# Rotary attention rows in two fp32r parts on half the array each, and a score tile of 640 keys cut as 384 + 256

## The chip, the core and the metric

The kernel runs on one core of a Trainium2 chip. The metric is the device time of one execution in microseconds (us). TensorE (PE in the rows, its weight loads PEld) multiplies, VectorE (DVE), ScalarE (ACT) and GpSimd (POOL) do the rest, and SyncE (SP) issues nearly all DMAs. The on-chip memory is SBUF, and TensorE writes to PSUM, which has 8 banks of 512 fp32 columns on 128 partitions.

## What is computed

A layer on x of 1024 tokens by 512 channels: a rotary attention of 32 heads of 16 channels, a feed-forward with experts, an attention with linear position biases (32 heads of 128, 8 key heads), and the feed-forward again, each with a residual. The change touches the first and, in one detail, the third.

```
def attention_fwd(x, wq, wk, wv, wo, n_heads=32):
    xq = rotary_pos_emb((x @ wq.T).reshape(B, T, n_heads, hd))
    xk = rotary_pos_emb((x @ wk.T).reshape(B, T, n_heads, hd))
    scores = jnp.einsum('bqhd,bkhd->bhqk', xq, xk) * scale
    scores = jnp.where(causal[None, None], scores, NEG_INF)
    probs = jax.nn.softmax(scores.astype(jnp.float32), axis=-1)
    out = jnp.einsum('bhqk,bkhd->bqhd', probs, xv).reshape(B, T, C)
    return out @ wo.T
```

## The kernel before

Products need nearly fp32 accuracy. [...] The kernel has these stages, one after the other:

**Rotary projection** (`rotary_projection_block`, L538, to about 131 us). For each of 8 token tiles TensorE makes q, k and v in 36 matmuls of 512 columns. ScalarE and VectorE apply the rotation into `rot`. The rotated rows are cut in three bf16 parts by casts and subtractions on ScalarE and VectorE (L671, L705, L675, L708), each part is transposed (L634, 24 transposes a tile), copied to `stage`, and stored to DRAM (`parts`) for two tiles at a time by SP (L581). From there SP loads them back into rows for scoring (L462): the rows of one head stand on 96 partitions, which hold the six products of parts in `A_TERMS`. Ones in three more partitions of `k_st` are made by GpSimd (L474), and the negated row maxima go into the same partitions of `q_st`, so a score matmul of 99 rows gives the score less its maximum.

**First maxima** (`FirstMaxima`). Heads go in 8 groups of 4. Row maxima of a group come from score pieces of up to 512 keys, 48 in a group: one matmul of 96 rows (L486, in the next stage L886), a matmul that adds the causal mask where the piece has the diagonal (L489, L889), and a VectorE reduction (L509, L989). Group 0 is done here.

**Rotary attention** (`rotary_attention_block`, L728, about 164 to 434 us). For each group 20 steps (`A_STEPS`). In a step TensorE scores one head's key blocks in a pair of banks (L914, and L918 for masks), ScalarE takes the exponent (L978), then come the products with v (`mix`, L932, four heads at once, each on 32 of the array's columns), and then the pieces for the maxima of the next group, on three banks (4, 5, 7). VectorE reduces the pieces. The order on TensorE is written out by hand; a piece waits until the reduction of the third piece before it has freed its bank, a score until the exponent two steps back is done:

```
for tau in range(NGA * S + 3):
    score(tau)
    ... mix(gg, k, n)
    ... piece(g + 1, n)
```

**Stream** (`stream_block`, about 434 to 1650 us): 64 steps of a token tile and a key head with 4 heads each. The keys of a tile are cut in spans of up to 512 by `key_spans`; a span of 128 is computed as 256 columns, since `score` takes `k0 = min(k0, k1 - 2 * P)`. VectorE adds the bias and takes the maximum of each span (L1754) in two banks. A feed-forward closes the kernel.

Of the kernel before, what the change touches and what calls it, by code (L numbers as in the profile page):

```python
# [411 lines left out]
A_PARTS = 3  # L412
A_ROWS = 6 * DA
A_UNITS = GA * NT
A_LINKS = 5
A_TERMS = ((0, 0), (0, 1), (0, 2), (1, 0), (1, 1), (2, 0))
A_PIECES = [(hh, i, c, span) for hh in range(GA) for i in range(NT) for c, span in enumerate(key_spans(i))]
A_FIRST = sorted(A_PIECES, key=lambda piece: piece[1])


class FirstMaxima:
# [5 lines left out]
    def __init__(self, nc, ctx, own, credited, const, ps, parts_dram):  # L427
# [7 lines left out]
        rows = sb("first_rows", [P, 4, GA * T], BF16)  # L435
        self.rows = rows
        self.q_st = [rows[:, 2 * b, :].rearrange("p (h t) -> p h t", h=GA) for b in range(2)]
        self.k_st = [rows[:, 2 * b + 1, :].rearrange("p (h t) -> p h t", h=GA) for b in range(2)]
# [3 lines left out]
        self.max_rest = sb("max_rest", [P, A_UNITS])  # L442
        self.max_part = sb("max_part", [P, A_PARTS, A_UNITS], BF16)
        self.max_rows = sb("max_rows", [P, P], BF16)
# [6 lines left out]
    def raw_weights(self):  # L451
        flat = self.rows[:, :, :].rearrange("p b n -> p (b n)").bitcast(F32)
        return [flat[:, k * 3 * C:(k + 1) * 3 * C] for k in range(KC)]

    def load_rows(self, queue, b, h, sides=(0, 1)):
        cols = slice(2 * h * P, 2 * (h + 1) * P)
        rows = [self.parts_dram[a].rearrange("(n g h d) t -> n g d h t", n=2, g=NGA, h=GA) for a in range(A_PARTS)]
        for s, (qa, ka) in enumerate(A_TERMS):
            at = slice(s * DA, (s + 1) * DA)
            for dst, n, a in ((self.q_st[b], 0, qa), (self.k_st[b], 1, ka)):  # L460
                if n in sides:
                    queue.dma_start(dst[at, :, cols], rows[a][n, b][:, :, cols]  # L462
                                    ).then_inc(self.loaded[1] if b else self.rows_in[h], 16)

    def store_max(self, sp):
        sp.wait_ge(self.credited["max_out"], 1 + 1)
        for a in range(A_PARTS):
            sp.dma_start(self.q_st[0][A_ROWS + a:A_ROWS + a + 1, :, :],
                         self.max_rows[a * A_UNITS:(a + 1) * A_UNITS, :]).then_inc(self.max_in[0], 16)

    def make_ones(self, pool):

        for b in range(2):
            pool.memset(self.k_st[b][A_ROWS:A_ROWS + A_PARTS, :, :], 1.0).then_inc(self.ones_made, 1)  # L474
            pool.wait_ge(self.ones_made, b + 1)

    def score_pieces(self, pe):
        pe.wait_ge(self.made, 2)
        for n, (hh, i, c, (k0, k1)) in enumerate(A_FIRST):
            if hh == 0 and c == 0 and i % 2 == 0:  # L480
                pe.wait_ge(self.rows_in[i // 2], 16 * 2 * len(A_TERMS))
# [4 lines left out]
            last = pe.matmul(out, self.q_st[0][0:A_ROWS, hh, i * P:(i + 1) * P], self.k_st[0][0:A_ROWS, hh, k0:k1],  # L486
# [6 lines left out]
    def turn_max(self, pe):  # L493
        pe.wait_ge(self.credited["link"], 1 + A_LINKS)
        pe.transpose(self.ps[0:A_PARTS * A_UNITS, 4, 0:P // 2].bitcast(BF16),
                     self.max_part[:, :, :].rearrange("p a u -> p (a u)"),
                     self.const["ident_bf"][:, :]).then_inc(self.credited["max_turned"], 1)
# [7 lines left out]
    def max_of_pieces(self, dve):  # L505
        for n, (hh, i, c, (k0, k1)) in enumerate(A_FIRST):
            u = hh * NT + i
# [4 lines left out]
    def split_max(self, dve, start=1, pieces_done=None):  # L512
# [6 lines left out]
        dve.scalar_tensor_tensor(self.max_rest[:, :], self.row_max[:, :], -1.0, self.max_part[:, 0, :],  # L519
                                 ALU.mult, ALU.subtract).then_inc(link, 1)  # L520
        dve.wait_ge(link, start + 3)
        dve.tensor_copy(self.max_part[:, 1, :], self.max_rest[:, :]).then_inc(link, 1)
        dve.wait_ge(link, start + 4)
        dve.tensor_tensor(self.max_part[:, 2, :], self.max_rest[:, :], self.max_part[:, 1, :],
                          ALU.subtract).then_inc(link, 1)

    def take_max(self, dve):
        dve.wait_ge(self.credited["max_turned"], 1 + 1)
        dve.tensor_copy(self.max_rows[0:A_PARTS * A_UNITS, :],
                        self.ps[0:A_PARTS * A_UNITS, 4, 0:P // 2].bitcast(BF16)).then_inc(self.credited["max_out"], 1)  # L530


def rotary_projection_block(nc, ctx, norm, weights, xt_h, xt_l, w_h, w_l, v_all, o_all, spare, stage_room, first, const, ps, parts_dram, x_in):
# [4 lines left out]
    with ExitStack() as own:  # L538
        def sb(name, shape, dt=F32):
# [5 lines left out]
        part = spare[:, 0:3 * 2 * C].bitcast(BF16).rearrange("p (b a n) -> p b a n", b=2, a=3)  # L545
        stage = [half.rearrange("p (a m t) -> p a m t", a=3, t=2 * P)
                 for half in (sb("stage", [P, 3 * 2 * KC * 2 * P], BF16)[:, :], stage_room.bitcast(BF16))]
# [4 lines left out]
        high_done = sem("high_done")  # L552
        rest1_done = sem("rest1_done")
        mid_done = sem("mid_done")
        low_done = sem("low_done")
        transposed = sem("transposed")
        staged_dve = sem("staged_dve")
        staged_act = sem("staged_act")
# [3 lines left out]
        def take_part(eng, copy, done, i, a):  # L562

            n = 3 * i + a
            eng.wait_ge(transposed, n + 1)
            if i % 2 == 0 and i >= 4:
                eng.wait_ge(stored[i // 2 % 2], 16 * 6 * (i // 4))
            copy(stage[i // 2 % 2][:, a, :, (i % 2) * P:(i % 2 + 1) * P],
                 ps[:, 6 + n % 2, :].bitcast(BF16).rearrange("p (m t) -> p m t", t=P)).then_inc(done, 1)
# [5 lines left out]

# [1452 lines left out]
```

## Time and profile before

| | us |
|---|---|
| median of 3 runs (1671.64 to 1673.54) | 1672.65 |
| the profiled execution | 1671.7 |
| its span | 1669.6 |
| TensorE busy | 1534.6 |
| VectorE busy | 1132.8 |
| ScalarE busy | 828.7 |
| GpSimd busy | 393.5 |

The profile is that of one execution. In its rows, a matmul's duration is modelled up to its last result, so matmuls overlap in time: the time that one takes from the engine is read from start to start.

### The profile page before, as it was taken

The numbers are of one execution on the slowest core, as the hardware profiler recorded it, in microseconds if no ns is written. First come the engines' busy times: TensorE is split into PE (matmuls) and PEld (weight loads), VectorE is DVE, ScalarE is ACT, GpSimd is POOL, SyncE is SP. The second block draws the span as 40 slices with busy tenths as digits, with TensorE's granted clock in tenths as the row PEclk, the third lists the DMA queues.
The fourth block names the chain that finished last, engine by engine and source line by source line (L and its number), as shares of the span: only waits on it lengthen the run. The fifth ranks groups of instructions, "written<-read, shape, count | busy, mean of one in ns | idle before, by whom it ended". The sixth has DMA issues, their size and how long they took to land. (4 is left out here: it accounts for less than half of the span.)

```text
span 1669.6 us, 25633 instructions
## 1 busy us (share of the span) xinstructions
PE 1534.6 (92%) x9096; PEld 1187.5 (71%) x9096; DVE 1132.8 (68%) x2845; ACT 828.7 (50%) x2104; POOL 393.5 (24%) x356
## 2 busy tenths in 40 slices
PE   3885999999898799999999999999999999999969
PEld 2772444443587688888888888888888888888757
DVE  5547777774375478677677677667767767867855
ACT  2451555556432455555555555556555555555521
POOL 4100100001253231322223133133133133131130
PEclk9996999999998899999999999999999999999979
DMA  3143533321100100100000010010010010000011
GB/s 144 38 115 93 73 40 39 43 36 53 44 27 1 38 14 14 39 7 20 14 26 26 1 38 26 1 39 26 1 38 26 1 39 14 13 1 1 1 45 51
DMA packets 42656, 54.56 MB, mean 33 GB/s; under 512 B 6304, under 2 KB 24992, under 8 KB 42528
## 3 DMA queue, kind: packets, MB, share of 16 engines
q1 hardware_dynamic: 41568, 52.52, 12.7%
q8 instruction: 73, 1.20, 0.3%
q10 hardware_dynamic: 960, 0.39, 0.1%
q14 instruction: 55, 0.45, 0.1%
HBM read 44.31 MB, written 8.39 MB: 32 GB/s over the span
## 5 line engine op out<-in xcount | busy, mean ns | idle before, releaser
L1649 ACT ACTIVATE prob<-prob,ab_neg_max 128x128 f32<-128x128 f32 (+7 forms) x256 | 201.5, 787 | 250.5 <-DVE ab_neg_max L1754 249.4
L1771 DVE TENSOR_TENSOR ab_pt_l<-ps,ab_pt_h 128x512 fp32r<-128x512 f32 x288 | 197.8, 687 | 74.0 <-ACT ab_pt_h L1677 73.1
L1677 ACT CAST ab_pt_h<-ps 128x512 fp32r<-128x512 f32 x288 | 171.6, 598 | 111.7 <-PE ps L1562 111.1
L1754 DVE CUSTOM_DVE_ANT_0 prob<-ps,rel 128x512 f32<-128x512 f32 (+3 forms) x256 | 150.3, 587 | 109.2 <-PE ps L52 108.5
L989 DVE TENSOR_REDUCE ra_part_max<-ps 128x1 f32<-128x128 f32 (+1 forms) x336 | 164.8, 550 | 49.7 <-PE ps L889 31.9
L50 PE MATMUL ps<-ab_w_h,ab_xt_h 128*128 128x512 f32 (+1 forms) x512 | 186.2, 364 | 4.3 <-DVE ab_v_l L1791 3.5
L1562 PE MATMUL ps<-ident,prob 128*128 128x128 f32 x1152 | 173.5, 273 | 5.8 <-DVE ab_qt_l L1763 4.5
L52 PE MATMUL ps<-ab_w_h,ab_xt_l 128*128 128x512 f32 (+1 forms) x512 | 173.9, 340 | 0.0
L51 PE MATMUL ps<-ab_w_l,ab_xt_h 128*128 128x512 f32 (+1 forms) x512 | 173.3, 338 | 0.0
L1779 DVE TENSOR_SCALAR prob<-prob,ab_recip 128x128 f32<-128x128 f32 (+7 forms) x256 | 165.8, 648 | 9.1
L1459 POOL TENSOR_TENSOR ab_rms<-ab_ms_eps,neg_half 128x5 f32<-128x5 f32 x64 | 77.7, 1214 | 341.1 <-DVE ab_ms_eps L1796 340.4
L1562 PEld LDWEIGHTS ps<-ident,prob 128*128 128x128 f32 x1152 | 138.1, 140 | 27.5 <-DVE ab_qt_l L1763 5.8
L978 ACT ACTIVATE ra_pt<-ps 128x1024 f32<-128x1024 f32 x96 | 97.3, 1024 | 103.6 <-PE ps L918 91.4
L50 PE MATMUL ps<-ab_kt_h,ab_qt_h 128*128 128x512 f32 (+2 forms) x384 | 135.5, 353 | 5.0 <-DVE ab_neg_max L1754 4.9
L52 PE MATMUL ps<-ab_kt_h,ab_qt_l 128*128 128x512 f32 (+2 forms) x384 | 134.1, 349 | 0.0
L51 PE MATMUL ps<-ab_kt_l,ab_qt_h 128*128 128x512 f32 (+2 forms) x384 | 133.8, 348 | 0.0
L50 PE MATMUL ps<-ab_pt_h,ab_v_h 128*128 128x512 f32 x288 | 128.0, 444 | 6.0 <-DVE ab_pt_l L1771 3.7
L1468 POOL CAST ab_o_h<-ab_o_raw 128x512 fp32r<-128x512 f32 x64 | 41.5, 649 | 348.1 <-ACT ab_o_raw L1691 314.0
L51 PE MATMUL ps<-ab_pt_l,ab_v_h 128*128 128x512 f32 x288 | 113.6, 395 | 0.0
L52 PE MATMUL ps<-ab_pt_h,ab_v_l 128*128 128x512 f32 x288 | 113.6, 394 | 0.0
L50 PEld LDWEIGHTS ps<-ab_w_h,ab_xt_h 128*128 128x128 f32 x512 | 97.4, 190 | 21.9 <-DVE ab_v_l L1791 8.3
L50 PE MATMUL ps<-wo,ab_o_h 128*128 128x512 f32 x256 | 102.6, 401 | 7.6 <-POOL ab_o_l L1470 7.6
(252 smaller groups left out, 3501.9 us busy)
## 6 DMA issues: line engine op xcount, KB each, us to landing
f_raw<-in_wqkv SPq DMA_DIRECT2D x32, 384.0 KB, 3.7
f_raw<-in_wbo SPq DMA_DIRECT2D x32, 256.0 KB, 2.6
ra_first_rows<-in_wa SPq DMA_DIRECT2D x4, 768.0 KB, 10.1
parts<-pa_stage SPq DMA_DIRECT2D x12, 256.0 KB, 3.4
parts<-f_raw SPq DMA_DIRECT2D x12, 256.0 KB, 3.4
ra_q_st<-parts SPq DMA_DIRECT2D x24, 128.0 KB, 6.1
ra_k_st<-parts SPq DMA_DIRECT2D x24, 128.0 KB, 6.7
ra_first_rows<-parts SPq DMA_DIRECT2D x24, 128.0 KB, 6.6
```

The costliest lines, as they stand in the source:

```text
L50: pe.matmul(out, lh, rh, start=start, stop=False)
L51: pe.matmul(out, lh, rl, start=False, stop=False)
L52: return pe.matmul(out, ll, rh, start=False, stop=stop)
L978: act.activation(pt[k % 3][:, h, :], pair.rearrange("p a b -> p (a b)"), ACT.Exp).then_inc(exped, 1)
L989: dve.tensor_reduce(part_max[:, c, u:u + 1], ps[:, PIECE_BANKS[n % len(PIECE_BANKS)], 0:k1 - k0], AX.X, ALU.max).then_inc(piece_max, 1)
L1459: pool.tensor_tensor(rms[:, t % 2, :], ms_eps[:, t % 2, :], const["neg_half"][:, 0:GB + 1], ALU.pow).then_inc(rms_ready, 1)
L1562: last = pe.transpose(ring_bank("p", u, j)[:, h * P:(h + 1) * P], prob[:, u % 2, h, j * P:(j + 1) * P], const["ident"][:, :])
L1649: act.activation(prob[:, t % 2, h, 0:w], prob[:, t % 2, h, 0:w], ACT.Exp, bias=neg_max[:, t % 2, h, pieces_per_head(t % NT) - 1:pieces_per ...
L1677: act.copy(pt_h[:, n % PT, :], ring_bank("p", u, j)).then_inc(pt_high, 1)
L1754: dve.tensor_tensor_reduce(out=prob[:, t % 2, h, k0:k1], in0=ps[:, n % 2, a:b], in1=const["rel"][:, SLIDE - i * P + k0:SLIDE - i * P + k1] ...
L1771: dve.tensor_tensor(pt_l[:, n % PT, :], ring_bank("p", u, j), pt_h[:, n % PT, :].bitcast(F32), ALU.subtract).then_inc(emptied, 1)
L1779: dve.tensor_scalar(prob[:, t % 2, h, 0:w], prob[:, t % 2, h, 0:w], recip[:, t % 2, h:h + 1], None, ALU.mult).then_inc(normed, 1)
```

## The change

The rotated q and k rows are kept in two fp32r parts in place of three bf16 ones, with three products of parts. A head's rows then take 48 partitions, 50 with the maxima, and a group's even heads stand on partitions 0 to 63 and its odd heads on 64 to 127. Scores and pieces become fp32r matmuls on 64 rows of the array. In each step the pieces are no longer given after the mix but in turn with the score blocks, and `piece_slots` chooses them so that they are of the other half; the masks, which use all 128 rows, follow each pair. The projection transposes `rot` itself in fp32 (8 transposes a tile) and makes the parts when it empties PSUM. `make_ones` fills whole `k_st` tiles. In the stream a tile of 640 keys is cut as 384 + 256 in place of 512 + 128.

```diff
-A_PARTS = 3
-A_ROWS = 6 * DA
+A_PARTS = 2
+A_TERMS = ((0, 0), (1, 0), (0, 1))
+A_ROWS = len(A_TERMS) * DA
+A_HALF = P // 2
-A_LINKS = 5
-A_TERMS = ((0, 0), (0, 1), (0, 2), (1, 0), (1, 1), (2, 0))
+A_LINKS = 3
+A_LOADS = 16 * 4 * len(A_TERMS)
+A_STORES = 16 * 2 * A_PARTS
-A_FIRST = sorted(A_PIECES, key=lambda piece: piece[1])
+A_FIRST = sorted(A_PIECES, key=lambda piece: (piece[1], piece[2]))
+def head_rows(st, hh, n):
+
+    at = A_HALF * (hh % 2)
+    return st[at:at + n, hh // 2, :]
+def store_maxima(queue, dst, max_rows, done):
+    for a in range(A_PARTS):
+        for r in range(2):
+            at = A_HALF * r + A_ROWS + a
+            src = a * A_UNITS + r * (A_UNITS // 2)
+            queue.dma_start(dst[at:at + 1, :, :].bitcast(F32), max_rows[src:src + A_UNITS // 2, :].bitcast(F32)).then_inc(done, 16)
...
         for b in range(2):
-            pool.memset(self.k_st[b][A_ROWS:A_ROWS + A_PARTS, :, :], 1.0).then_inc(self.ones_made, 1)
+            pool.memset(self.k_st[b][:, :, :].bitcast(F32), 1.0).then_inc(self.ones_made, 1)
...
             def turn(i):
-                pe.wait_ge(low_done, i + 1)
-                for a in range(3):
-                    n = 3 * i + a
...
-                    for m in range(2 * KC):
-                        last = pe.transpose(ps[:, 6 + n % 2, m * 64:(m + 1) * 64].bitcast(BF16),
-                                            part[:, i % 2, a, m * P:(m + 1) * P], const["ident_bf"][:, :])
+                pe.wait_ge(rot_done, i + 1)
+                for n in range(2):
+                    if i:
+                        pe.wait_ge(staged_low, 2 * (i - 1) + n + 1)
+                    for m in range(KC):
+                        last = pe.transpose(ps[:, 6 + n, m * P:(m + 1) * P],
+                                            rot[:, i % 2, (n * KC + m) * P:(n * KC + m + 1) * P], const["ident"][:, :])
                     last.then_inc(transposed, 1)
...
+            def take_high(i):
+                stage_free(act, i)
+                for n in range(2):
+                    act.wait_ge(transposed, 2 * i + n + 1)
+                    act.copy(staged(i, n, 0).bitcast(F32R),
+                             ps[:, 6 + n, :].rearrange("p (m t) -> p m t", m=KC)).then_inc(staged_high, 1)
...
+def piece_slots(slots):
+
+
+    by_tile = sorted(A_PIECES, key=lambda piece: (piece[1], piece[2]))
+    queues = [[p for p in by_tile if p[0] % 2 == 1], [p for p in by_tile if p[0] % 2 == 0]]
+    order, ends = [], [0]
+    for t in range(slots):
+        queue = queues[t % 2]
+        left = len(range(t, slots, 2))
+        size = sum(k1 - k0 + W // 4 for _, _, _, (k0, k1) in queue)
+        taken = 0
+        while queue and taken * left < size:
+            order.append(queue.pop(0))
+            k0, k1 = order[-1][3]
+            taken += k1 - k0 + W // 4
+        ends.append(len(order))
+    return order, ends
...
+            def mask_piece(n):
+                hh, i, c, (k0, k1) = PIECES[n]
+                if k1 == P * (i + 1):
+                    pe.matmul(ps[:, PIECE_BANKS[n % len(PIECE_BANKS)], k1 - k0 - P:k1 - k0], const["ident_bf"][:, :],
+                              mask[:, :], start=False, stop=True).then_inc(piece_scored, 1)
...
+                for x in range(max(len(blocks), len(pieces))):
+                    if x < len(blocks):
+                        m, j, q0, col = blocks[x]
                         own_keys = kind != "full"
...
+                        last = pe.matmul(out, head_rows(k_st[b], h + m, ROWS)[:, j * P:(j + 1) * P],
+                                         head_rows(q_st[b], h + m, ROWS)[:, half * W + q0:(half + 1) * W],
                                          start=True, stop=not own_keys)
+                    if x < len(pieces):
+                        piece(group, pieces[x])
+                    if x < len(blocks):
                         if own_keys:
                             last = pe.matmul(out[:, 0:P], mask[:, :], const["ident_bf"][:, :], start=False, stop=True)
+                        if x == len(blocks) - 1:
+                            last.then_inc(scored, 1)
+                    if x < len(pieces):
+                        mask_piece(pieces[x])
...
+def score_spans(i):
+
+    w = P * (i + 1)
+    at = min(w, W if w - W != P else W - P)
+    return [(0, at)] + ([(at, w)] if w > at else [])
```

Three places show how instructions move on TensorE. The first is step 1 of a middle group in the rotary attention (half 0, head 1, with the masks of its three key blocks); the column count at a row's end is that of the moving operand. Before, the score blocks with their masks come first, then two mixes, then the pieces:

```order
L914 MATMUL ps<-ra_q_st,ra_k_st 128x512
L918 MATMUL ps<-ident_bf,ra_mask 128x128
L914 MATMUL ps<-ra_q_st,ra_k_st 128x384
L918 MATMUL ps<-ident_bf,ra_mask 128x128
L914 MATMUL ps<-ra_q_st,ra_k_st 128x128
L918 MATMUL ps<-ident_bf,ra_mask 128x128
L932 MATMUL ps<-ra_pt,ra_v 32x128 x4
L932 MATMUL ps<-prob,ra_v 32x256 x4
L886 MATMUL ps<-ra_first_rows 128x384
L889 MATMUL ps<-ra_mask,ident_bf 128x128
L886 MATMUL ps<-ra_first_rows 128x512
```

In the changed kernel the same step (L916 is the score matmul, L881 the piece, L923 and L890 the masks, L940 the mix) reads:

```order
L916 MATMUL ps<-ra_q_st,ra_k_st 128x512
L881 MATMUL ps<-ra_first_rows 128x128
L923 MATMUL ps<-ident_bf,ra_mask 128x128
L890 MATMUL ps<-ra_mask,ident_bf 128x128
L916 MATMUL ps<-ra_q_st,ra_k_st 128x384
L881 MATMUL ps<-ra_first_rows 128x512
L923 MATMUL ps<-ident_bf,ra_mask 128x128
L916 MATMUL ps<-ra_q_st,ra_k_st 128x128
L881 MATMUL ps<-ra_first_rows 128x512
L923 MATMUL ps<-ident_bf,ra_mask 128x128
L940 MATMUL ps<-ra_pt,ra_v 32x128 x4
L940 MATMUL ps<-prob,ra_v 32x256 x4
```

Each score block now has a piece behind it, both on 64 rows of the array, and behind these a mask or two on 128 rows. The masks stand between the pairs.

The second place is the projection between two tiles. Before:

```order
L50 MATMUL ps<-a_w_h,wo 128x512
L51 MATMUL ps<-a_w_l,wo 128x512
L52 MATMUL ps<-a_w_h,a_xt_l 128x512
L634 MATMUL ps<-ident_bf,prob 128x128 x24
L50 MATMUL ps<-a_w_h,wo 128x512
```

In the changed kernel `L631 MATMUL ps<-ident,prob 128x128 x8` stands where the row of 24 stood, and the rows around it are the same.

The third is the score of a tile of 640 keys in the stream. Before, the head's two spans, with a part of the projection between them:

```order
L50 MATMUL ps<-ab_kt_h,ab_qt_h 128x512
L51 MATMUL ps<-ab_kt_l,ab_qt_h 128x512
L52 MATMUL ps<-ab_kt_h,ab_qt_l 128x512
...
L50 MATMUL ps<-ab_kt_h,ab_qt_h 128x256
L51 MATMUL ps<-ab_kt_l,ab_qt_h 128x256
L52 MATMUL ps<-ab_kt_h,ab_qt_l 128x256
```

In the changed kernel the first three rows have 384 columns and the last three stay at 256. That is so for 32 heads, 96 matmuls in all; no row of the stream moves to another place.

## Rows read from the trace of the kernel before

**Rows 1.** The page: the span, and TensorE's busy time, share and instructions.

```profile
span 1669.6 us, 25633 instructions
PE 1534.6 (92%) x9096; PEld 1187.5 (71%) x9096; DVE 1132.8 (68%) x2845; ACT 828.7 (50%) x2104; POOL 393.5 (24%) x356
```

**Rows 2.** Windows: length, busy PE, PEld, DVE, ACT, POOL, PEclk, DMA share, GB/s.

```profile
192.00:226.00 34.00, 32.35 (x267) 14.82 (x265) 25.80 (x59) 19.51 (x22) 0.61 (x1) 1.00 0.38 48
396.00:432.00 36.00, 31.65 (x277) 12.34 (x275) 2.15 (x8) 26.14 (x30) 3.71 (x4) 1.00 0.19 61
```

**Rows 3.** Waits from 200 to 360 us: total us, times, longest.

```profile
PEld ps L886 <- DVE ra_part_max L989: 47.9, 97, 0.8
```

**Rows 4.** Timeline, TensorE: start, us, instruction, count.

```profile
258.13 0.22 PE L889 MATMUL ps<-ra_mask,ident_bf 128*128 128x128 bf16 x1
258.19 0.60 PE L914 MATMUL ps<-ra_q_st,ra_k_st 99*128 99x512 bf16 x2
258.72 1.07 PE L932 MATMUL ps<-prob,ra_v 128*32 128x512 f32 x8
259.71 0.60 PE L914 MATMUL ps<-ra_q_st,ra_k_st 99*128 99x512 bf16 x2
260.25 1.06 PE L932 MATMUL ps<-prob,ra_v 128*32 128x512 f32 x8
```

**Rows 5.** Timeline, TensorE: fp32 transposes, then bf16 scores.

```profile
244.96 0.60 PE L941 MATMUL ps<-ident,ra_o_rows 128*128 128x128 f32 x4
245.41 0.38 PE L914 MATMUL ps<-ra_q_st,ra_k_st 99*128 99x512 bf16 x1
```

**Rows 6.** Timeline, VectorE; then a group of lines (ScalarE): count, busy us, mean ns.

```profile
149.07 9.12 DVE L509 TENSOR_REDUCE ra_part_max<-ps 128x1 f32<-128x512 f32 x16 [4.03 <-PE ps L486]
L978 ACT ACTIVATE ra_pt<-ps 128x1024 f32<-128x1024 f32 x54 | 54.9, 1024 | 41.6 <-PE ps L918 35.1 <-PE ps L914 6.4
```

**Rows 7.** Timeline, TensorE, in the projection between two tiles.

```profile
68.97 0.40 PE L52 MATMUL ps<-a_w_h,a_xt_l 128*128 128x512 f32 x1
69.20 1.07 PE L634 MATMUL ps<-ident_bf,prob 128*128 128x128 bf16 x16
70.61 0.62 PE L634 MATMUL ps<-ident_bf,prob 128*128 128x128 bf16 x8 [0.34 <-DVE pa_stage L568]
71.04 0.48 PE L50 MATMUL ps<-a_w_h,wo 128*128 128x512 f32 x1
71.36 0.40 PE L51 MATMUL ps<-a_w_l,wo 128*128 128x512 f32 x1
```

**Rows 8.** Timeline, GpSimd, VectorE and TensorE, ahead of the second tile.

```profile
35.40 0.54 DVE L158 TENSOR_SCALAR prob<-x,an_mean_var,an_rstd 128x512 f32<-128x512 f32 x1
39.79 7.41 POOL L474 MEMSET ra_first_rows<- 3x4096 bf16 x2
44.27 3.22 DVE L158 TENSOR_SCALAR prob<-x,an_mean_var,an_rstd 128x512 f32<-128x512 f32 x1
50.61 0.50 PE L50 MATMUL ps<-a_w_h,wo 128*128 128x512 f32 x1 [1.40 <-DVE a_xt_l L163]
```

**Rows 9.** Timeline, SP's queue: start, us of issue, DMA, count.

```profile
77.08 4.14 SPq L581 DMA_DIRECT2D parts<-pa_stage  x6
124.81 11.11 SPq L462 DMA_DIRECT2D ra_first_rows<-parts  x24
136.01 4.23 SPq L581 DMA_DIRECT2D parts<-f_raw  x6
142.95 5.48 SPq L462 DMA_DIRECT2D ra_first_rows<-parts  x12
```

**Rows 10.** Timeline, TensorE, in the stream.

```profile
800.18 0.39 PE L52 MATMUL ps<-ab_w_h,ab_xt_l 128*128 128x512 f32 x1
800.41 0.28 PE L50 MATMUL ps<-ab_w_h,ab_xt_h 128*128 128x256 f32 x1
800.53 0.28 PE L51 MATMUL ps<-ab_w_l,ab_xt_h 128*128 128x256 f32 x1
```

More of the change, by code:

```diff
@@ L485, in score_pieces @@
             last_span = k1 == P * (i + 1)
-            last = pe.matmul(out, self.q_st[0][0:A_ROWS, hh, i * P:(i + 1) * P], self.k_st[0][0:A_ROWS, hh, k0:k1],
+            last = pe.matmul(out, head_rows(self.q_st[0], hh, A_ROWS)[:, i * P:(i + 1) * P],
+                             head_rows(self.k_st[0], hh, A_ROWS)[:, k0:k1],
                              start=True, stop=not last_span)
@@ L598, in _ @@
             weights.split_low(pool)
-            pool.wait_ge(weights.w_low, KC)
             first.make_ones(pool)
@@ L795, in pieces_before @@
         def pieces_before(t):
[L797 to L802 removed]
+            return PIECES_TO[min(t, LAST_PIECE)]
         def jobs_at(tau, lag):
@@ L849, in _ @@
         def _(pool):
+            for b in range(2, A_BUFS):
+                pool.memset(k_st[b][:, :, :].bitcast(F32), 1.0).then_inc(ones_made, 1)
+                pool.wait_ge(ones_made, b + 1)
             for b in range(2):
@@ L883, in piece @@
                     pe.wait_ge(max_out, count(1, g, 0))
-                out = ps[:, PIECE_BANKS[n % len(PIECE_BANKS)], 0:k1 - k0]
                 last_span = k1 == P * (i + 1)
-                last = pe.matmul(out, q_st[b][0:A_ROWS, hh, i * P:(i + 1) * P], k_st[b][0:A_ROWS, hh, k0:k1],
-                                 start=True, stop=not last_span)
-                if last_span:
-                    last = pe.matmul(out[:, k1 - k0 - P:k1 - k0], const["ident_bf"][:, :], mask[:, :],
-                                     start=False, stop=True)
@@ L891, in piece @@
-                last.then_inc(piece_scored, 1)
+                last = pe.matmul(ps[:, PIECE_BANKS[n % len(PIECE_BANKS)], 0:k1 - k0],
+                                 head_rows(q_st[b], hh, A_ROWS)[:, i * P:(i + 1) * P],
+                                 head_rows(k_st[b], hh, A_ROWS)[:, k0:k1], start=True, stop=not last_span)
+                if not last_span:
+                    last.then_inc(piece_scored, 1)
+            def mask_piece(n):
[3 more added lines that the diff above has]
+                              mask[:, :], start=False, stop=True).then_inc(piece_scored, 1)
@@ L900, in score, with score_and_pieces @@
+            def score_and_pieces(tau, group, pieces):
                 g, t = tau // S, tau % S
                 b = g % A_BUFS
-                k, h = A_STEPS[t]
-                kind, half, _ = A_SETS[k]
-                if t == 0:
-                    pe.wait_ge(max_in[b], 16 * A_PARTS * (g // A_BUFS + 1))
-                    pe.wait_ge(ones_made, min(g, A_BUFS - 1) + 1)
-                pe.wait_ge(exped, 1 + max(0, tau - 1))
-                for m in range(2 if kind == "rest" else 1):
-                    for j, q0, col in blocks_a(k):
-                        n = W - q0
+                blocks = []
+                if g < NGA:
+                    k, h = A_STEPS[t]
+                    kind, half, _ = A_SETS[k]
+                    if t == 0:
+                        pe.wait_ge(max_in[b], A_STORES * (g // A_BUFS + 1))
+                    pe.wait_ge(exped, 1 + max(0, tau - 1))
+                    blocks = [(m, *block) for m in range(2 if kind == "rest" else 1) for block in blocks_a(k)]
+                for x in range(max(len(blocks), len(pieces))):
+                    if x < len(blocks):
+                        m, j, q0, col = blocks[x]
@@ L946, in _ @@
                 piece(1, n)
+                mask_piece(n)
             for tau in range(NGA * S + 3):
-                g, t = tau // S, tau % S
-                if g < NGA:
-                    score(tau)
+                g, t = (tau + SHIFT) // S, (tau + SHIFT) % S
+                score_and_pieces(tau, g + 1, range(pieces_before(t), pieces_before(t + 1)) if g + 1 < NGA else ())
+                if g + 1 < NGA and t == MAX_AT:
+                    turn_max(g + 1)
                 for gg in range(NGA):
```

219 lines of the change are left out of this document (82 added, 137 removed).

## Prediction

> **What bounds the kernel now.** I read the page first: TensorE is busy 92% of the span, VectorE 68% [rows 1]. Then the windows by stage, since most of the change lies in the rotary attention. In a middle group's 34.0 us (its rows repeat after that time) TensorE is busy 32.35 and VectorE 25.80; in the last group, which has no pieces, 31.65 of 36 us and 2.15 [rows 2]. So TensorE bounds the groups by its work. The view of waits shows the rest: pieces wait 97 times, 47.9 us in all, for a bank that VectorE frees [rows 3], each for at most 0.8 us. A step is bound by TensorE or, where it has many pieces, by VectorE.
>
> TensorE's prices, from start to start. Two score matmuls of 512 columns take 0.53 us in front of a mix and 0.54 behind one; a 128-column mask takes 0.06 (258.13 to 258.19); the mix of a key block, four heads side by side on 32 columns of the array, takes 0.99 (258.72 to 259.71) [rows 4]. I count bf16 at 0.215 for 512 columns. Then two scores should take 0.43; so the change to the mix's shape and back costs the 0.10 behind the scores, and 0.99 less 0.85 (8 records of 512 fp32 columns, two to each quarter, at two cycles a column and 2.4 GHz) is 0.14: 0.24 for a round trip. A change of type alone costs nothing: four fp32 transposes take 0.45, and the bf16 score follows at once [rows 5]. An fp32r matmul takes 0.23 for 512 columns and 0.12 for 256 [rows 10], or 0.32 where its weight load shows (71.04 to 71.36) [rows 7].
>
> Check on before: per group, scores and pieces have 36,864 columns (15.5 us), 64 masks 3.6, mixes 7.7, ten visits to mixes 2.4, transposes 0.9: 30.1, where 32.35 is busy by modelled ends. If each of the 20 steps takes the larger of TensorE's work, VectorE's reductions (16 in 9.12 us, so about 0.57 for the widest, and less for narrower ones) and ScalarE's exponent (1.02) [rows 6], it is 33.1. Measured is 34.0, so 0.9 is waiting between.
>
> **The change in the groups.** *What it removes.* A piece and a score of opposite halves could run at once. Summed over the order, with the longer of each pair, 36,864 columns become 26,496. At fp32r's 0.45 us per 1000 that is 11.9 in place of 15.5: 3.6 us less a group, if the halves overlap. No row shows two row halves at once; the nearest is the mix, where four column quarters take 0.99 for 4096 fp32 columns on all of them, so they do overlap [rows 4].
>
> *What it adds.* The masks use all 128 rows. In a group there are 55 places of a pair (or a single matmul); behind 43 of them stands a mask, so the array goes from halves to full rows and back 43 times. No row shows that change. Bounds: below nothing, as with a change of type [rows 5]; above 0.33, the mix's 0.24 [rows 4] and 0.09 of exposed fp32r weights [rows 7]. The nearest row is the mix's: a change of the array's shape between two plain matmuls. I take 0.24 each, less 0.12 at the ten mixes, whose own change is then partly made already: 43 × 0.24 − 1.2 = +9.1 on TensorE. TensorE's sum becomes 26.5 + 9.1 = 35.6 against 30.1.
>
> The Trainium skill ("TensorEngine Tiling (Array Packing)", Tiling Modes, Key Properties) says that tiles run independently, and that changing the tiling mode, not just the tile, drains TensorE. The trace agrees for the mix's columns (the 0.24 above); no row here shows it for rows.
>
> *What else moves.* VectorE's reductions are as many as before, 24.3 us a group, ScalarE's as well. The pieces now come with the scores, not behind the mix: a piece that waits for VectorE holds the score blocks behind it, then the mix, and by `scored` the exponent, so ScalarE starts later. Step by step with the larger of the three engines, a group gives 32.0 us at a price of 0, 33.3 at 0.10, 35.0 at 0.16, 37.7 at 0.24, 41.3 at 0.33, against 33.1 for before. So the sign turns near 0.09 by steps and near 0.11 by TensorE's sum (3.6 + 1.2 over 43) where VectorE covers nothing; the waits of the 0.9 that may go raise it to about 0.17. The forecast: +2.6 (before's gap of 3.9 between sum and measured vanishes by two thirds as TensorE fills up: 35.6 + 1.0 − 34.0) to +4.6 (37.7 − 33.1), taken +3.6 a group, ×7 = **+25**.
>
> The last group has no pieces to overlap, and its masks still change the mode. By steps: 25.1 before, 25.3 at 0, 29.9 at 0.24, 32.8 at 0.33: **+4.8**.
>
> fp32r of 128 columns: 16 pieces and some scores a group. No row shows one below 256 columns. Below it costs nothing, since most stand beside a wider partner; above, if 128 cost what 256 does (0.12 [rows 10]), 16 × 0.06 on singles, at most +0.4 a group. I take nothing.
>
> **Projection and first maxima.** 24 bf16 transposes start at 69.20 and, with a break, end before 71.04: 1.84 us [rows 7]. Eight fp32 ones take twice the 0.45 of four [rows 5]: 0.9. That is −0.94 a tile, −6.6 for seven tiles on TensorE.
>
> GpSimd's two memsets (3 × 4096 bf16) take 7.41, 0.90 ns a column. Beside them VectorE's `tensor_scalar` takes 3.22 in place of 0.54, and TensorE waits for that chain [rows 8]. After, two of 2048 fp32 columns: I take the price by columns, 3.7, so −3.7. If it goes by bytes, 7.4: nothing gained.
>
> But SP's queue nearly fills the time too: stores to loads 6.94 (136.01 to 142.95), 24 loads 11.11, together 18.05 [rows 9]. The parts grow from 1.5 to 2 MB for two tiles (4 stores of 512 KB), the loads stay 24: about 8.0 + 11.1 = 19.1, more than TensorE's new pair of tiles (its rounds take 58.93/3 = 19.64 now [rows 9], less 1.9). So SP sets the end. First stores: 77.08 − 3.7 − 1.9 − 3.1 (one pass less on each of ScalarE and VectorE before the parts are there, about 1.0 each for 1024 columns [rows 6], and one hand-over of about as much, an estimate) = 68.4; three rounds of 19.1 put the last ones at 125.7 against 136.01. Then one longer store, +1, and in the first maxima mode changes +1 and four stores of maxima for three, less two links, 0: **−8**. Bounds: −2 (memset by bytes and no shorter chain) to −11.
>
> **Stream.** 96 matmuls lose 128 columns of fp32r: 0.23 − 0.12 for 256 [rows 10], so 0.055 to 0.057 each. TensorE bounds there; the later span is unchanged and VectorE's two maxima become more even. **−5.4** (bounds −6 to 0).
>
> **Sum.** 25 + 4.8 − 8 − 5.4 = +16.4 on the profiled execution's own 1671.7: 1688; the median of the runs is 1 us above it, so 1689.
>
> **Rivals.** (a) *The halves' change is free, and pairs overlap.* For it: type changes are free [rows 5], and a half array stays two halves of the same columns, unlike the mix. Against it: rows 4. A group then changes by −1.1 (steps), −3.6 (TensorE's sum) or, with the 0.9 and better spread pieces, −4.7. With −13.4 outside and 0 in the last group: 1651, 1634, 1626; centre 1638. This ends on the other side, and decides below a price of about 0.10.
>
> (b) *About half the price, 0.12:* the modelled 0.10 in front of the mix [rows 4] is all, and the way back hides under the next weights. +0.7 a group by steps, +2.3 last: 4.9 + 2.3 − 13.4, less up to 3 for freed waits: 1665 (1650 to 1675).
>
> (c) *Dearer:* 0.33, with fp32r weights exposed (+7.3 × 7 + 7.7 − 13.4 = +45, 1717), or halves that don't overlap: at 0.24 a group gives 41.2, and about the same time. Against it: in a step of 1.7 us VectorE's and ScalarE's work covers part.
>
> The Trainium skill ("TensorE: Matmul & The Clock Gate", Part 3) gives a measured speedup of 3.07 for four row tiles at 512 columns. By a like share (0.77 of ideal), two halves would save less than the 3.6 above, about 2.3; no row here shows it.
>
> **How the numbers follow.** Forecast (0.24; 1675 to 1708): 0.42. (a) 0.32, (b) 0.16, (c) 0.10. The range leaves out the dearest part of (c) and the lowest third of (a): 1632 to 1712; the forecast's own is 1675 to 1708. 0.2% (3.3 us) is about what a measurement of this kernel can tell from no change. Faster: all of (a) and three quarters of (b), 0.44; same 0.06 from the rest of (b) and the forecast's edge; slower 0.50.
>
> **What would show it.** In the windows of a middle group: its length (37.6 forecast; 30 to 33 under (a)), and TensorE's start to start from a pair over its mask to the next score, which under the forecast is 0.24 longer than the columns. A piece and a score that start within 0.1 us of each other and end together show the overlap. The mask row after a pair shows the drain. In the projection: eight transposes in 0.9, the memsets' time and `tensor_scalar` beside them, SP's stores near 68 and 126. In the stream a span of 384 in 0.17. The prediction is wrong by the most if the change of rows is free, and next if VectorE, not TensorE, holds the steps.

## The result and the profile after

The changed kernel takes 1859.3 us in the median of 4 runs (1853.8 to 1864.0), the kernel before 1672.1 (1671.6 to 1673.5): ratio 1.1116, 95% interval 1.1096 to 1.1136. The sign was as forecast, the size was not: +187 us where +16 was said, and outside the range.

The page of the changed kernel, its span, busy times, and the granted clock in 40 slices, in tenths of full speed:

```profile
span 1853.4 us, 25330 instructions
PE 1746.4 (94%) x8968; PEld 1258.6 (68%) x8968; DVE 1133.3 (61%) x2821; ACT 807.6 (44%) x2088; POOL 385.8 (21%) x356
PEclk9975565567655799999999999999999999999989
```

The same line of the kernel before:

```profile
PEclk9996999999998899999999999999999999999979
```

TensorE has 128 fewer instructions than in [rows 1] and is busy 212 us longer. The clock line shows what changed: from the third slice to the fourteenth the changed kernel has digits of 5 to 7, where the kernel before has one below 8 in that stretch. The working of the prediction has no term for this.

The time by marks that both traces have. GpSimd copies the next group's v rows when a group is mixed, so its rows beat the groups. Before (start, us, engine, line, instruction):

```profile
208.67 0.61 POOL L858 COPY ra_v<-v_all 128x512 f32<-128x512 f32 x1 [35.54 <-PE ps L932]
...
378.62 0.61 POOL L858 COPY ra_v<-v_all 128x512 f32<-128x512 f32 x1 [33.40 <-PE ps L932]
```

After:

```profile
242.19 0.61 POOL L859 COPY ra_v<-v_all 128x512 f32<-128x512 f32 x1 [81.34 <-PE ps L940]
...
529.12 0.61 POOL L859 COPY ra_v<-v_all 128x512 f32<-128x512 f32 x1 [59.33 <-PE ps L940]
```

| stretch | before | after | difference |
|---|---|---|---|
| start to the first stores of maxima | 159.99 | 150.61 | −9.4 |
| to the v copy of the third group | 48.7 | 91.6 | +42.9 |
| five groups | 169.95 | 286.93 | +117.0 |
| last groups, to the stream's first transposes | 56.6 | 96.8 | +40.2 |
| stream and feed-forward | 1234.4 | 1227.5 | −6.9 |

The sum is +183.8, the difference of the two spans. Everything outside the groups went nearly as forecast; all of the loss is in the rotary attention, some 200 us over its three stretches and 23 us in each of the five groups between the marks.

Windows of the changed kernel: a whole group, then twelve microseconds at half clock and eight at full clock in it (columns as in [rows 2]):

```profile
242.19:300.08 57.89, 57.89 (x267) 22.72 (x267) 28.41 (x56) 19.82 (x23) 0.61 (x1) 0.62 0.18 28
299.00:311.00 12.00, 12.00 (x53) 5.40 (x45) 5.80 (x13) 3.98 (x6) 0.61 (x1) 0.50 0.01 2
263.00:271.00 8.00, 8.00 (x46) 3.41 (x45) 4.30 (x13) 5.67 (x6) 0.00 (x0) 1.00 0.02 4
```

TensorE is busy in every microsecond of the group and yet has a mean clock of 0.62, where [rows 2] has 1.00. So the busy share of the records doesn't tell whether the clock holds. The rise comes once a group and at the same place in it (261, 319, 377 and 435 us), for 14 to 20 us each.

The first groups met a clock that was already down. It fell at 114 us, in the projection, and stayed at half through the first maxima (TensorE was busy for 35.9 of the 46 us to 160). The kernel before is at half ahead of its groups too, from 157 us on, but is back at full from 174; the changed one gets there at 261 us, without a gap in TensorE's work from 160 us on:

```profile
160.00:260.00 100.00, 100.00 (x378) 39.22 (x382) 48.37 (x92) 26.13 (x29) 1.46 (x3) 0.50 0.19 28
```

TensorE's timeline of the changed kernel at half clock (1.2 GHz), a mix and then a part of a step:

```profile
253.79 1.94 PE L940 MATMUL ps<-ra_pt,ra_v 128*32 128x512 f32 x8
255.66 0.79 PE L916 MATMUL ps<-ra_first_rows 50*128 50x512 f32 x1
...
305.70 0.47 PE L916 MATMUL ps<-ra_q_st,ra_k_st 50*128 50x128 f32 x1
305.71 0.79 PE L881 MATMUL ps<-ra_k_st,ra_q_st 48*128 48x512 f32 x1
306.43 0.29 PE L923 MATMUL ps<-ident_bf,ra_mask 128*128 128x128 bf16 x1
306.65 0.58 PE L916 MATMUL ps<-ra_q_st,ra_k_st 50*128 50x256 f32 x1
```

And at full clock (2.4 GHz):

```profile
263.06 0.49 PE L916 MATMUL ps<-ra_first_rows 50*128 50x512 f32 x1
263.07 0.50 PE L881 MATMUL ps<-ra_k_st,ra_q_st 48*128 48x512 f32 x1
263.50 0.23 PE L890 MATMUL ps<-ra_mask,ident_bf 128*128 128x128 bf16 x1
263.66 0.49 PE L916 MATMUL ps<-ra_first_rows 50*128 50x512 f32 x1
```

A score and a piece of opposite halves start within 0.01 us and take the time of the longer one: they overlap in full. Over the prices that the prediction used, 0.23 for 512 columns and 0.06 for a mask, the round trip from halves to all rows and back costs (263.50 − 263.06) − 0.23 = 0.21 into the mask and (263.66 − 263.50) − 0.06 = 0.10 out of it at full clock: 0.31 where 0.24 was taken. The section on e8 shows what that is made of. And at half clock the same stretch, a pair with 512 columns as the longer part and one mask, takes 0.94 (0.72 to the mask, 0.22 behind it) in place of 0.60, the mix 1.87 (253.79 to 255.66) in place of 0.99 [rows 4].

The front and the stream, which the prediction reached by [rows 7 to 10]. TensorE in the projection, then SP's queue:

```profile
101.35 1.03 PE L631 MATMUL ps<-ident,prob 128*128 128x128 f32 x8
102.14 0.48 PE L50 MATMUL ps<-a_w_h,wo 128*128 128x512 f32 x1
```

```profile
68.38 0.93 SPq L585 DMA_DIRECT2D parts<-a_stage  x2
...
126.26 0.42 SPq L585 DMA_DIRECT2D parts<-prob  x1
...
150.61 2.51 SPq L449 DMA_DIRECT2D ra_first_rows<-ra_max_rows  x4
```

Eight transposes take 0.79 (0.9 was taken); the first stores stand at 68.4 and the last ones at 126.3, where the working had 68.4 and 125.7. That they agree so closely is in part luck: GpSimd's two memsets take 4.11 us (3.7 was taken), and TensorE reaches the second tile at 47.70 us, 2.9 earlier than before (50.61 [rows 8]), where 3.7 was taken.

### The profile page after: what moved, and what is told of

It is laid out like the page before. It is cut to its first block and busy times, and to the rows that moved or that the text cites. A ratio compares the mean times of both kernels' runs of the same rounds, so it can differ in the third digit from the quotient of the medians.

```text
span 1853.4 us, 25330 instructions
## 1 busy us (share of the span) xinstructions
PE 1746.4 (94%) x8968; PEld 1258.6 (68%) x8968; DVE 1133.3 (61%) x2821; ACT 807.6 (44%) x2088; POOL 385.8 (21%) x356
## 3 DMA queue, kind: packets, MB, share of 16 engines
q1 hardware_dynamic: 32224, 54.68, 11.2%
## 5 line engine op out<-in xcount | busy, mean ns | idle before, releaser
L993 DVE TENSOR_REDUCE ra_part_max<-ps 128x1 f32<-128x512 f32 (+1 forms) x336 | 184.3, 556 | 191.0 <-PE ps L890 145.6
L1764 DVE CUSTOM_DVE_ANT_0 prob<-ps,rel 128x512 f32<-128x512 f32 (+3 forms) x256 | 145.9, 570 | 101.7 <-PE ps L52 101.0
L881 PE MATMUL ps<-ra_k_st,ra_q_st 48*128 48x512 f32 (+3 forms) x192 | 113.2, 597 | 0.0
```

The source lines that it names most:

```text
L881: last = pe.matmul(ps[:, PIECE_BANKS[n % len(PIECE_BANKS)], 0:k1 - k0], head_rows(q_st[b], hh, A_ROWS)[:, i * P:(i + 1) * P], head_rows(k_ ...
L993: dve.tensor_reduce(part_max[:, c, u:u + 1], ps[:, PIECE_BANKS[n % len(PIECE_BANKS)], 0:k1 - k0], AX.X, ALU.max).then_inc(piece_max, 1)
L1764: dve.tensor_tensor_reduce(out=prob[:, t % 2, h, k0:k1], in0=ps[:, n % 2, a:b], in1=const["rel"][:, SLIDE - i * P + k0:SLIDE - i * P + k1] ...
```

## Experiments

The question was now why the clock falls in the groups. Two things are new there that could leave the array less to do: it stands still at each change of row mode, that is, between matmuls on half of the rows and matmuls on all of them (**drains**), and a matmul works on 48 to 50 of its 128 rows (**rows**). e1, e3, e4, e6, e8 and e10 are one execution each.

### e1: without masks

```diff
-                        own_keys = kind != "full"
+                        own_keys = False
...
-                    pe.matmul(ps[:, PIECE_BANKS[n % len(PIECE_BANKS)], k1 - k0 - P:k1 - k0], const["ident_bf"][:, :],
-                              mask[:, :], start=False, stop=True).then_inc(piece_scored, 1)
```

> The changed kernel without the causal masks behind scores and pieces in the rotary attention (its output then takes in future keys; exponents are scaled down so that they stay finite). No change between half rows and full rows is left there but those around the mix. Theory drains (the array's standing still at each change of row mode is what keeps TensorE at 1.2 GHz): granted clock in the groups back at 1.00 and a group of about 30 to 32 us where the changed kernel has 57.9, total near 1655. Theory rows (the few rows in use, 48 to 50 of 128 in a matmul, keep it there): clock stays at 0.6, a group of about 45 us, total near 1760.

Measured: 1707.5 us. Two groups of its windows:

```profile
203.55:238.14 34.59, 32.84 (x203) 14.89 (x205) 25.39 (x57) 19.44 (x24) 0.62 (x1) 0.85 0.30 47
238.14:283.23 45.09, 44.42 (x203) 20.37 (x205) 26.36 (x57) 19.73 (x24) 0.62 (x1) 0.55 0.24 37
```

Neither theory's numbers came: most of the loss goes (57.9 to 34.6 and 45.1 us a group), but even with no mode change but those at mixes and transposes, the clock doesn't hold. Drains matter, and something else does too.

### e2: each mask on its own half

The right result with no change of row mode but those at mixes and transposes. A mask of 128 rows is made as two matmuls of 64 rows and 64 columns, on the half on which its block stands:

```diff
+def add_mask(pe, out, own_mask, own_at, ident_bf, hh):
+    at = A_HALF * (hh % 2)
+    rows = slice(at, at + A_HALF)
+    for s in range(2):
+        last = pe.matmul(out[:, A_HALF * s:A_HALF * (s + 1)], own_mask[rows, own_at[s]:own_at[s] + P],
+                         ident_bf[rows, rows], start=False, stop=s == 1)
+    return last
...
-                            last = pe.matmul(out[:, 0:P], mask[:, :], const["ident_bf"][:, :], start=False, stop=True)
+                            last = add_mask(pe, out[:, 0:P], mask, MASK_AT, const["ident_bf"], h + m)
```

> The changed kernel with each mask made on the block's own half of the rows, as two matmuls of 64 rows and 64 columns, in the first maxima too. Same results, same pairs, no row-mode change but those around mix and transposes. Theory drains: granted clock 1.00, a group of 31 to 33 us, total 1640 to 1660, faster than the kernel before. Theory rows: clock stays at 0.5 to 0.65, a group of 45 to 50 us, total 1760 to 1800.

Measured: 1719.9 us median of 4 runs, 1694.5 to 1735.0. The runs differ by their clock (0.938 in the shortest, 0.911 in the longest); the ratio of 1.020 (1.013 to 1.027) is over the two shorter ones. Windows of two groups in one execution:

```profile
209.98:242.11 32.13, 31.43 (x331) 17.75 (x331) 25.59 (x57) 19.38 (x23) 0.61 (x1) 1.00 0.35 52
281.73:328.21 46.48, 46.38 (x331) 25.16 (x331) 26.89 (x56) 19.73 (x23) 0.62 (x2) 0.61 0.25 36
```

One of its falls, with 0.40 us of idle time in the 14 us ahead of it and none behind it:

```profile
248.00:262.00 14.00, 13.60 (x139) 7.30 (x136) 10.17 (x25) 9.99 (x11) 0.00 (x0) 1.00 0.07 18
262.00:309.00 47.00, 47.00 (x285) 24.13 (x286) 24.64 (x48) 17.13 (x20) 0.62 (x1) 0.50 0.24 31
```

Without these mode changes and at full clock the paired order gives 32.1 us a group: what rival (a) of the prediction had by steps (32.0). But the same instructions also run at 0.61 and then take 46.5. 140 us of the changed kernel's 187 are gone, and since a group at full clock is shorter than before's 34.0, what is left of the loss in the groups is clock. Each theory had one clock for all groups (1.00, or 0.5 to 0.65), and neither was right.

### e3 and e4: many rows against few, without mode changes

```diff
-    at = A_HALF * (hh % 2)
-    return st[at:at + n, hh // 2, :]
+    return st[0:A_HALF + n, hh // 2, :]
```

That is e3, with 112 to 114 rows. In e4 the new line is `return st[0:66, hh // 2, :]`.

> The changed kernel with every score and piece contracted over 112 or 114 rows, both heads' at once (it computes the sum of two heads' scores, exponents scaled down; q rows are cleared first by a memset of GpSimd that the changed kernel doesn't have). All matmuls then use the full array: no row-mode change, and no overlap either. Order and columns as in the changed kernel. Theory drains: clock 1.00, group 35 to 37 us. Theory rows: clock 1.00 as well, group 35 to 37.

> As e3, but over 66 rows: the full array's mode with about half of its rows in use (it scores the even head's rows and two more for both heads). No row-mode change, no overlap. Theory drains: same as e3, clock 1.00, group 35 to 37 us. Theory rows: clock 0.5 to 0.7 in the groups, group 50 to 60 us. So the pair e3 and e4 tells the count of rows apart from the changes of mode.

Measured: e3 1687.6 us, e4 1769.5. Windows of e3, a group:

```profile
250.33:286.88 36.55, 36.31 (x266) 20.37 (x267) 26.31 (x56) 19.63 (x23) 0.62 (x2) 1.00 0.27 46
```

Windows of e4, an early group and a late one, then the stretches before and after its clock rises:

```profile
240.12:305.33 65.21, 65.21 (x266) 34.95 (x266) 28.88 (x56) 19.82 (x23) 0.61 (x1) 0.50 0.18 25
392.23:428.70 36.47, 36.21 (x266) 20.37 (x267) 26.30 (x56) 19.59 (x23) 0.61 (x1) 1.00 0.30 45
119.00:337.00 218.00, 203.66 (x798) 115.12 (x798) 111.40 (x222) 53.74 (x60) 10.57 (x12) 0.50 0.23 42
338.00:507.00 169.00, 166.14 (x1222) 92.31 (x1220) 106.62 (x228) 94.29 (x107) 9.82 (x12) 1.00 0.25 42
```

The two kernels have the same instructions in the same order; only the rows of scores and pieces differ. With 112 to 114 rows the clock is back at full at 178 us, and every group from the second on takes 36.5 us at 1.00. With 66 rows it stays at half, where it has been since 119 us in the projection, until 337 us (a group takes 65.2), and then at full to the end of the groups (36.5). So few rows were enough to keep the clock from rising, with no mode change but those at mixes and transposes, and the state lasts: the same group runs in either. But they didn't make it fall: once at full, e4's clock held for 169 us, where e2's fell again, with 98 to 100 rows in a pair. The count of rows is a part of the cause and not all of it; what else e2 has isn't known.

### e8: many rows, with mode changes

The other corner: the kernel before, whose scores and pieces have 96 to 99 rows, with its masks over 64 rows, so that each mask changes the row mode.

```diff
-                    last = pe.matmul(out[:, k1 - k0 - P:k1 - k0], const["ident_bf"][:, :], mask[:, :],
+                    last = pe.matmul(out[:, k1 - k0 - P:k1 - k0], const["ident_bf"][0:P // 2, :], mask[0:P // 2, :],
...
-                            last = pe.matmul(out[:, 0:P], mask[:, :], const["ident_bf"][:, :], start=False, stop=True)
+                            last = pe.matmul(out[:, 0:P], mask[0:P // 2, :], const["ident_bf"][0:P // 2, :], start=False, stop=True)
```

> The kernel before, its masks in the rotary attention over rows 0 to 63 only (the mask of the lower 64 rows is left out, exponents scaled down): 64 changes to half rows and back in a group with the scores' 96 to 99 rows left as they are. Theory rows: clock stays at 1.00 and a group grows by 64 times the price of a round trip at full clock, 0.2 to 0.25 us less what other waits cover: 44 to 48 us for 34.0. Theory drains (the changes alone pull the clock down): clock near 0.6, a group of 60 us or more.

Measured: 1829.8 us. Windows of a group:

```profile
284.00:338.37 54.37, 54.37 (x266) 18.38 (x265) 27.35 (x58) 19.74 (x22) 0.61 (x2) 0.74 0.25 30
```

TensorE's timeline of e8 where the clock is at 2.4 GHz:

```profile
250.08 0.39 PE L886 MATMUL ps<-ra_k_st,ra_q_st 96*128 96x512 bf16 x1
250.41 0.23 PE L889 MATMUL ps<-ra_mask,ident_bf 64*128 64x128 bf16 x1
250.56 0.39 PE L886 MATMUL ps<-ra_k_st,ra_q_st 96*128 96x512 bf16 x1
```

The clock falls to 0.74 here (0.81 in the group ahead of it) with the rows of scores and pieces as before: drains alone pull it down. There are 64 round trips a group, more than the changed kernel's 43, and the clock is still above its 0.62. Few rows don't explain that, since e10 below has them filled up and 0.62 as well; the cause of the difference is open.

A round trip costs 0.33 − 0.215 = 0.115 in and 0.15 − 0.06 = 0.09 out, 0.21. The changed kernel's 0.31 is 0.10 more. Most of that isn't the change of mode, for e3, in which masks, scores and pieces all use the full array, has it too. Its PE and PEld rows:

```profile
330.85 0.23 PE L891 MATMUL ps<-ra_mask,ident_bf 128*128 128x128 bf16 x1
330.85 0.20 PEld L917 LDWEIGHTS ps<-ra_first_rows 114*128 114x128 f32 x1
330.89 0.48 PE L917 MATMUL ps<-ra_first_rows 114*128 114x512 f32 x1
331.21 0.39 PE L882 MATMUL ps<-ra_first_rows 112*128 112x512 f32 x1
...
332.65 0.40 PE L882 MATMUL ps<-ra_first_rows 112*128 112x512 f32 x1
332.89 0.40 PE L917 MATMUL ps<-ra_first_rows 114*128 114x512 f32 x1
```

An fp32r matmul (fp32r is the type of the high and low parts) of 512 columns takes 0.24 behind another one and 0.32 behind a mask, which is too short to cover its weight load of 0.20. So a mask and such a matmul take 0.04 + 0.32 = 0.36 in e3 without a change of mode and 0.16 + 0.44 = 0.60 in the changed kernel with it. The change itself is 0.24 there, and 0.07 of the 0.31 are the weights of fp32r.

### e5 and e10: rows filled up with zeros

```diff
-    ROWS = A_ROWS + A_PARTS
+    ROWS = A_HALF
...
+            pool.memset(self.q_st[b][:, :, :].bitcast(F32), 0.0)
             pool.memset(self.k_st[b][:, :, :].bitcast(F32), 1.0).then_inc(self.ones_made, 1)
```

Scores then have 64 rows a half in place of 50, pieces 62 in place of 48, with the maxima in the last two rows. e5 does it in e2, e10 in the changed kernel.

> e2 (masks on their own half) with every score over 64 rows and every piece over 62: rows of zeros in q and ones in k fill the half, and the maxima stand in the last two rows. Same results. Theory rows as instructed (the clock goes by the rows that matmuls address): pairs now use 126 to 128 of 128 rows where e2's use 98 to 100, so the clock stays at 1.00, a group takes 32 to 33 us in all groups, total near 1650. Theory rows with data (only rows whose values change the sum count): as e2, groups of 32 to 46 us, total 1695 to 1735.

> The changed kernel (masks on 128 rows, so the row mode changes 43 times in a group) with its scores and pieces padded to 64 and 62 rows with zeros, as e5. With the changed kernel, e2 and e5 it makes the square of two causes. If either alone is enough to keep the clock down: a group near 57.9 us, total near 1860. If the two add up, rows giving back what they gave between e2 and e5: clock 0.8 to 0.9 in the groups, a group of 42 to 50 us, total 1760 to 1810. Bound if the clock holds: 38 to 39 us a group by the mode changes at full clock.

Measured: e5 1674.6 us median of 10 runs (1665.4 to 1685.9), ratio 1.0025 (0.9997 to 1.0053); e10 1848.9. Windows of two neighbouring groups of e5:

```profile
244.67:276.77 32.10, 31.41 (x331) 17.75 (x331) 25.57 (x57) 19.36 (x23) 0.61 (x2) 1.00 0.32 52
276.77:310.19 33.42, 32.73 (x331) 18.33 (x331) 25.63 (x57) 19.36 (x23) 0.61 (x1) 0.95 0.35 50
```

And of e10:

```profile
412.36:470.31 57.95, 57.95 (x267) 22.58 (x267) 28.45 (x56) 19.68 (x23) 0.61 (x2) 0.62 0.20 29
```

Where there are no drains but the mix's, the padded rows give back 45 us: no run of e5 is as long as the shortest of e2 (the kernel before took 1671.7 and 1671.6 beside them). The padding adds nothing but rows whose products are zero, zeros of q times ones of k, and with them the clock holds in most groups. It still isn't certain: it dips for some microseconds, and the runs spread by 20 us. Where the drains stay, the same padding gives nothing in the groups (57.95 against 57.9), so the two causes don't add up: the drains alone hold this kernel's clock at 0.62. e5 missed the 1650 that was expected of it, and not in its undisturbed groups: the v copy of its third group stands at 212.5 us, 3.9 later than before (208.7).

### e6: pieces beside scores of their own half

```diff
-    queues = [[p for p in by_tile if p[0] % 2 == 1], [p for p in by_tile if p[0] % 2 == 0]]
+    queues = [[p for p in by_tile if p[0] % 2 == 0], [p for p in by_tile if p[0] % 2 == 1]]
```

> The changed kernel with the two queues of pieces exchanged, so that pieces come beside scores of their own half: same matmuls, same masks and mode changes, no pairs. If pairs overlap as the trace of the changed kernel reads (a score and a piece start within 0.01 us and end together), a group grows from 57.9 us by about 10,368 columns at 1.2 GHz, 8 to 9 us, less what VectorE covers: 64 to 68 us, total 1900 to 1930. If the overlap is only in the records: 57.9 as before.

Measured: 1973.8 us. A group, by the windows:

```profile
253.62:328.32 74.70, 74.70 (x266) 32.26 (x267) 28.99 (x56) 19.85 (x23) 0.61 (x1) 0.50 0.14 22
```

The overlap is real: the group grows by 16.8 us, where 6 to 10 were expected. 8.6 of them are the 10,368 columns at 1.2 GHz. The rest fits the clock, which now never rises (0.50 for 0.62): the 13.9 us that the changed kernel runs at full clock in a group would take some 23 at half.

### e7: the stream's spans alone

```diff
-            k0, k1 = key_spans(i)[c]
+            k0, k1 = score_spans(i)[c]
```

> The kernel before with only the stream's spans changed to 384 + 256. 96 matmuls of 128 columns less: 5.4 us less, ratio 0.9968; if VectorE's maxima or ScalarE's work bound those tiles, 0 to 2 us.

Measured: 1666.0 us in the median of 6 runs, ratio 0.9969 (0.9957 to 0.9982): −5.2 by the ratio and −5.7 by the medians, the term of the prediction (−5.4).

### e9 and e11: what can be kept

e9 is e7 with one more line, e11 is e5 with it and with the other two buffers' memsets behind the first copy of v:

```diff
+            pool.wait_ge(projected, 1)
             first.make_ones(pool)
```

> The kernel before with the stream's spans of 384 + 256, and with GpSimd's memset of ones held back until the first token tile is projected, so that VectorE's normalisation doesn't run beside it. Spans 5.7 us as measured alone; VectorE's tensor_scalar back from 3.2 to 0.54 us each beside it, and TensorE at its second tile 2 to 4 us earlier, which the first store and all behind it follow: 1662 to 1665, ratio 0.994 to 0.996. If ScalarE or another chain holds the second tile: 1666 as with the spans alone.

> e5 (masks on own half, padded rows) with GpSimd's memsets held back: those of the first two buffers until the first tile is projected, those of the other two until the v rows of two groups are copied. Front 4 to 6 us shorter than e5's, groups 32.1 us at full clock as in e5: 1658 to 1665 where the clock holds, up to 1680 where it drops for some stretches; median 1667.

Measured: e9 1662.6 us (1660.2 to 1664.2), ratio 0.9948 (0.9934 to 0.9961). e11 1660.5 us median (1659.6 to 1682.5), ratio 0.9935 (0.9921 to 0.9948) over five of its six runs, without the one of 1682.5. VectorE in e9, beside no memset now:

```profile
39.58 0.53 DVE L158 TENSOR_SCALAR prob<-x,an_mean_var,an_rstd 128x512 f32<-128x512 f32 x1
```

Both beat both kernels, by about half a per cent. They can't be told apart in the median, but five runs of e11 lie within 1.6 us and the sixth is 22 us longer; a window of that one shows a group of 35.4 us at a clock of 0.89. e9 has groups of 34.0 at 1.00 in all and is the one to keep.

## Why the prediction was wrong

**What failed** is in the part on the groups: every price there was taken at the clock of [rows 2], 1.00, for a kernel that gives TensorE other work. The step "TensorE's sum becomes 26.5 + 9.1 = 35.6" held only if the clock stayed, and no rival let it go. What the runs showed in its place is a clock of 0.62 in the groups, and 57.9 us a group where 37.6 was forecast. How much of that is the clock can be worked out, though no run shows it apart. In the changed kernel's group the mean clock of 0.62 means 0.76 of 57.9 us at half clock, 44 us. At full clock its pairs would take 0.60/0.94 and its mixes 0.99/1.87 of their time, some 0.6 together: 26.4 + 13.9 = 40.3 us a group. So of the 23.9 us that a group lost, about 6.3 is its work at full clock (mode changes and weights, less the columns saved) and 17.6 the clock. Over eight groups the clock is then some 140 to 150 us, and the whole kernel at full clock would take 1710 to 1720, by estimate: near rival (c) and at or above the upper end of the range.

**Why the clock fell.** In the changed kernel's groups TensorE had no idle time ahead of the falls (at 274, 333 and 391 us none in the 14 us before). What it had were row-mode changes (e8: 0.74 with nothing else changed in kind) and few rows (e4: 0.50 for 218 us, e2: falls in some groups, both with the mode changes of mixes and transposes alone). e3, with neither, holds 1.00 in the groups; e5, with filled rows and no more mode changes than e2, nearly does; the changed kernel and e10 have the drains and stay at 0.62. So the drains are the larger cause: without them (e2) 140 us come back, by filling the rows alone (e10) 10.

**Point by point.**
- *The halves overlap:* right, in full (e6, and the starts of pairs). A pair loses nothing of its factor of two, so the share of 0.77 that was set beside the sum from the Trainium skill ("TensorE: Matmul & The Clock Gate", Part 3) isn't seen here. At full clock a pair takes 0.24 up to a mask on its own half (e5, 286.35 to 286.59 in the rows at the end), as one matmul on the full array does (e3, above), and at half clock a lone piece of 512 columns in front of a mask (162.88 to 163.60 in the timeline below) takes the 0.72 of a pair.

```profile
162.88 0.79 PE L881 MATMUL ps<-ra_first_rows 48*128 48x512 f32 x1
163.60 0.29 PE L890 MATMUL ps<-ra_mask,ident_bf 128*128 128x128 bf16 x1
```

- *A row-mode change costs 0.24:* the mechanism was right, and so was the size (0.24, and 0.21 in e8). Too small was the term as a whole, 0.31 a round trip: the weights of fp32r, 0.07 each by e3, which were kept for rival (c) with 0.09, show behind every mask. That is 3 us a group. By the steps of the prediction 0.31 gives about 40.4 us a group at full clock. The Trainium skill ("TensorEngine Tiling (Array Packing)", Tiling Modes, Key Properties) says that a change of mode drains TensorE; the runs agree, with 0.21 in e8 and 0.24 here.
- *VectorE covers part of it:* not shown. TensorE has no idle time in a group, at half clock or at full.
- *The last group, +4.8:* with the end of the one before it, +40.2, at half clock for 76 of the 97 us.
- *Projection and first maxima, −8:* −9.4 to the first stores of maxima. SP's queue set its rounds, as said (loads up to 87.72, the next store at 87.77). The first maxima's pieces also ran at half clock, with 11.2 of 16 us busy on TensorE (134 to 150 us), so it cost little there.
- *Stream, −5.4:* −5.2 by e7.
- *Rival (a):* its condition was false here, but its size was right: e2's 32.1 us where no row-mode change is left and the clock holds.

## What to carry to other kernels

Before a change that makes matmuls smaller in rows or alternates their shape, ask what the granted clock will do, and give the case in which it falls a chance and a price: TensorE's share at up to twice its time (65.2 for 36.5 us in e4). A busy share of 100% is no assurance; look at the clock of the windows first. Look also at what state the stage ahead leaves the clock in. If halves of the array are to be paired, keep everything between the pairs on halves too (here a mask of two 64-row matmuls), and let each matmul address all rows of its half, with zeros if need be. Where fp32r matmuls stand behind short ones, add what of their weights shows.

## What the runs showed of the hardware

- Two fp32r matmuls on opposite halves of the rows run at once at no cost: in e5 a pair of 512 columns takes 0.24 up to the mask on its own half. The pair ahead of it takes 0.34 with the same columns, because it is the first behind a mix: its matmuls last 0.50 in place of 0.39. On the full array the first one behind a mix does the same (0.34, then 0.24 and 0.24 in e3), so that isn't a price of halves:

```profile
285.22 0.86 PE L965 MATMUL ps<-ra_pt,ra_v 128*32 128x128 f32 x16
286.01 0.50 PE L941 MATMUL ps<-ra_q_st,ra_k_st 64*128 64x512 f32 x1
286.01 0.73 PE L906 MATMUL ps<-ra_first_rows 62*128 62x512 f32 x2
286.35 0.39 PE L941 MATMUL ps<-ra_q_st,ra_k_st 64*128 64x512 f32 x1
286.59 0.23 PE L460 MATMUL ps<-ident_bf,ra_mask_t 64*128 64x64 bf16 x2
```

- The granted clock falls to half while TensorE's records leave no gap, by changes of row mode alone: e8 is busy throughout from 248 to 312 us, with 1.00 up to 271 and 0.50 from 272. Few rows can keep it at half (e4, 0.50 up to 337 us) where 112 to 114 rows don't (e3).
- The state lasts: e4's same group takes 65.2 us in one state and 36.5 in the other, and e2's 46.5 and 32.1, each in one execution. Kernels whose clock comes and goes spread from run to run: 40 us in e2, 20 in e5, where the kernel before spreads by 4.
- Rows that only add products of zero help to hold the clock (e5's 1674.6 against e2's 1719.9).
- VectorE's `tensor_scalar` takes 3.22 us beside GpSimd's memset of 3 partitions in bf16 [rows 8], 1.50 beside the changed kernel's memset of 128 partitions in fp32, and 0.53 without (e9).
